# Ranking in pieces between VectorE's wide steps, with bucket numbers compared from PSUM, in a two-layer graph kernel

## The reference

```python
h = relu(layernorm(x))
x = x + segment_sum((h * node_vec1)[src], dst, 12500) * node_vec1_n2                     # layer 0
h = relu(layernorm(x))
x = x + (1 + eps) * h + segment_sum(relu(h[src] + edge_attr_32), dst, 12500)             # layer 1
```

## Time and profile before

| | us |
|---|---|
| median of 3 runs | 4801.34 |
| lowest, highest | 4799.08, 4803.71 |
| the profiled execution | 4791.23 |
| its span, first to last instruction | 4789.2 |

### The profile page before, as it was taken

One profiled execution on the slowest core, in us unless ns is written; L12 is line 12 of the kernel. 1 busy time (PEld: TensorE's weight loads), 2 busy tenths in 40 slices (PEclk: granted clock), 3 DMA queues, 4 the chain that ended last, 5 costly groups with the idle time before them and its releaser, 6 DMA issues.

```text
span 4789.2 us, 130194 instructions
## 1 busy us (share of the span) xinstructions
PE 3721.2 (78%) x43852; PEld 2888.9 (60%) x43852; DVE 3812.7 (80%) x11454; ACT 3261.3 (68%) x9090; POOL 3497.5 (73%) x3590
## 2 busy tenths in 40 slices
PE   0388888888888888888888899467767777777775
PEld 0266666666666666666666666356666666666664
DVE  9788888888888888888888886767777776777775
ACT  1377777777777777777777777456666766666664
POOL 6757777777777777777777777477777777777774
PEclk9999999999999999999999999778888888888887
DMA  6322222222222222222222221211212221211221
GB/s 111 63 51 54 57 54 54 54 56 54 54 54 56 54 53 54 56 54 53 54 56 54 53 54 44 72 39 54 57 43 54 57 57 54 58 49 48 57 57 26
DMA packets 439702, 262.77 MB, mean 55 GB/s; under 512 B 334660, under 2 KB 423732, under 8 KB 432632
## 3 DMA queue, kind: packets, MB, share of 16 engines
q1 hardware_dynamic: 322488, 187.55, 16.7%
q0 software_dynamic: 110816, 60.69, 6.7%
q10 hardware_dynamic: 5728, 5.82, 0.5%
HBM read 172.96 MB, written 80.85 MB: 53 GB/s over the span
## 4 chain that ended last, share of the span: by engine, by line
PE 32%; POOL 23%; DVE 19%; issue 13%; ACT 10%; DMA 2%; DVEq 1%; ACTq 0%; SPq 0%; POOLq 0%
POOL stage L759 22%; PE candidates L1247 18%; PE plain_ps L1259 7%; DVE arena L1753 7%; ACT message L987 5%; DVE arena L1729 4%; ACT centered L956 2%; PE sorted_agg L1187 2%; PE candidates L1157 1%; ACT arena L880 1%; POOL message L759 1%; PE key_rows L1230 1%; DMA stage<-in_edge_attr 1%; DVE counts L1475 1%; PE key_rows L1139 1%
## 5 line engine op out<-in xcount | busy, mean ns | idle before, releaser
L771 POOL DMA_INDIRECT records<-stage,place_i x1875 | 1879.0, 1002 | 696.2 <-issue 652.0
L759 POOL DMA_INDIRECT stage<-table,src_plain x1250 | 1246.9, 997 | 409.1 <-issue 377.3
L987 ACT ACTIVATE message<-candidates,member_is 128x96 bf16<-128x96 f32 x4560 | 1170.7, 377 | 429.4 <-PE candidates L1247 426.3
L1753 DVE TENSOR_SCALAR arena<-window_iota,dst_rel 128x224 bf16<-128x224 f16 (+1 forms) x4800 | 1091.2, 302 | 37.8
L880 ACT ACTIVATE arena<-key_rows 125x640 f16<-125x640 f16 x1000 | 653.2, 716 | 215.1 <-DVE arena L1729 83.2
L1187 PE MATMUL sorted_agg<-arena 128*96 128x224 bf16 (+1 forms) x5000 | 654.1, 285 | 161.0 <-DVE arena L1753 109.6
L1259 PE MATMUL plain_ps<-summed,message 128*96 128x224 bf16 x4560 | 609.2, 269 | 68.2 <-ACT message L987 68.2
L1187 PEld LDWEIGHTS sorted_agg<-arena 128*96 128x96 bf16 x5000 | 543.7, 137 | 186.1 <-issue 118.6
L1259 PEld LDWEIGHTS plain_ps<-summed,message 128*96 128x96 bf16 x4560 | 490.7, 128 | 269.6 <-ACT message L987 127.4
L1729 DVE TENSOR_SCALAR arena<-arena,row_key 125x1280 bf16<-125x1280 f16 x1000 | 554.7, 555 | 96.5 <-ACT arena L880 64.6
L1139 PE MATMUL key_rows<-ident,record 128*125 128x128 f16 x5000 | 425.8, 235 | 239.2 <-DMA record<-records 96.2
(11 more groups left out here) (228 smaller groups left out, 5139.0 us busy)
## 6 DMA issues: line engine op xcount, KB each, us to landing
record<-records SPq DMA_DIRECT2D x50, 1650.0 KB
stage<-in_edge_attr SPq DMA_DIRECT2D x125, 400.0 KB, 3.2
records<-pad SPq DMA_DIRECT2D x25, 1650.0 KB, 11.9
records<-stage,place_i POOLq DMA_INDIRECT x1875
stage<-table,src_plain POOLq DMA_INDIRECT x1250
message<-table,mid_src POOLq DMA_INDIRECT x288
xs<-in_x SPq DMA_DIRECT2D x8, 390.6 KB
table<-parts ACTq DMA_DIRECT2D x4, 585.9 KB
```

The lines of the kernel that those rows point to most:

```text
L759: pool.indirect_dma_start(message[:, k, j, :] if l == 0 else rows[:, k, j, :], None, table0 if l == 0 else table1, bass.IndirectOffsetOnAx ...
L771: pool.indirect_dma_start(records, bass.IndirectOffsetOnAxis(ap=place_i[:, h, e:e + 1], axis=0), stage[:, h, e, :], None).then_inc(scatter ...
L987: last = nc.scalar.activation(direct_message[n % DB][:, m * WIDE:(m + 1) * WIDE], candidates[n % 2][:, m * WIDE:(m + 1) * WIDE], ACT.Copy, ...
L1753: last = nc.vector.tensor_scalar(dst_onehot(g, t), window_iota[:, 0:WA if tile == 0 else WT], dst_rel[:, h, tile:tile + 1], None, ALU.is_e ...
```

## The change

`rank_within` is split in two for the batches of the loop. `rank_buckets` (the small steps and the three comparisons) follows step 2's `direct_onehots`, `rank_scans` of one unit each follows those of steps 2, 3 and 4, and `rank_sums` and `rank_places` follow those of step 6, ahead of the last wide step. TensorE's `prefixes` moves from ahead of step 6 to ahead of step 5. The bucket numbers that the comparison reads were float16 in SBUF and are now float32 in PSUM, in 75 columns of a bank that layer 0 uses for nothing but the scans' constant operand. To make room there, the scans go over 17, 17 and 16 buckets where they went over 20, 20 and 10; there are nine as before.

```diff
-        bucket16 = sb("bucket16", [P, SE], F16)
...
-        SCANNED = 20
+        SCANNED = 17
         goes_on = sorted_agg[1][:, 0:SCANNED * J]
+        bucket_ps = sorted_agg[1][:, SCANNED * J:SCANNED * J + SE]
...
-                            if n == FIRST[SUBS - 2] and left_after(b) >= 2:
+                            if n == FIRST[SUBS - 3] and left_after(b) >= 2:
                                 prefixes(b + 2)
...
             def rank_within(b, h, u):
+                rank_buckets(b, h, u)
+                for v in range(SORTED):
+                    rank_scans(b, v)
...
-                step(nc.vector.tensor_copy(bucket16[:], bucket_of[:]))
+                step(nc.vector.tensor_copy(bucket_ps, bucket_of[:]))
...
                     step(nc.vector.tensor_tensor(
                         in_bucket[:, v, :].rearrange("p (g j) -> p g j", j=J), bucket_iota[:],
-                        bucket16[:, v * J:(v + 1) * J].unsqueeze(1).to_broadcast([P, BUCKETS, J]), ALU.is_equal))
...
+                        bucket_ps[:, v * J:(v + 1) * J].unsqueeze(1).to_broadcast([P, BUCKETS, J]), ALU.is_equal))
...
+            def rank_scans(b, v):
...
+                for some in SCANS:
+                    last = nc.vector.tensor_tensor_scan(counts[:, v, some], goes_on[:, 0:some.stop - some.start],
+                                                        in_bucket[:, v, some], 0.0, ALU.mult, ALU.add)
...
                             direct_onehots(b, h, s)
-                            if s == SUBS - 3 and more:
-                                rank_within(b + 2, h, u + 1)
-                        if more:
-                            rank_sums(b + 2)
-                            rank_places(b + 2, h, u + 1)
+                            if s == 2 and more:
+                                rank_buckets(b + 2, h, u + 1)
+                            if s in (2, 3, 4) and more:
+                                rank_scans(b + 2, s - 2)
+                            if s == SUBS - 2 and more:
+                                rank_sums(b + 2)
+                                rank_places(b + 2, h, u + 1)
                         first_onehots(*after(b, h, u))
```

More of the change, by code:

```diff
@@ L1429, in rank_within, with rank_buckets @@
             def rank_within(b, h, u):
+                rank_buckets(b, h, u)
+                for v in range(SORTED):
+                    rank_scans(b, v)
+            def rank_buckets(b, h, u):
                 nth = [0]
@@ L1448, in rank_within, with step @@
                         in_bucket[:, v, :].rearrange("p (g j) -> p g j", j=J), bucket_iota[:],
-                        bucket16[:, v * J:(v + 1) * J].unsqueeze(1).to_broadcast([P, BUCKETS, J]), ALU.is_equal))
[L1450 to L1457, removed]
+                        bucket_ps[:, v * J:(v + 1) * J].unsqueeze(1).to_broadcast([P, BUCKETS, J]), ALU.is_equal))
+                assert nth[0] == 8 + SORTED
+            def rank_scans(b, v):
+                nth = [8 + SORTED + v * len(SCANS)]
+                def step(ins):
+                    nth[0] += 1
+                    ins.then_inc(rank1_steps, 1)
+                    dve.wait_ge(rank1_steps, b * RANK1 + nth[0])
+                for some in SCANS:
+                    last = nc.vector.tensor_tensor_scan(counts[:, v, some], goes_on[:, 0:some.stop - some.start],
+                                                        in_bucket[:, v, some], 0.0, ALU.mult, ALU.add)
+                    if v < SORTED - 1 or some != SCANS[-1]:
+                        step(last)
+                if v == SORTED - 1:
+                    last.then_inc(scans_ready, 1)
+                    assert nth[0] == RANK1
             HALVINGS = []
```

## The result

| | before | after |
|---|---|---|
| median of 4 runs each, us | 4802.32 | 4957.22 |
| lowest, highest | 4799.08, 4803.71 | 4954.49, 4963.40 |
| ratio | | 1.0325 [1.0307, 1.0343] |
| span of the profiled execution | 4789.2 | 4956.5 |

The change costs 155 us; forecast were 154. In the profile after, L1447 is L1452 (comparison), L1452 is L1465 (scans), L1475 is L1489 (sums), L1516 is L1530 (last of the places), L1729 is L1743, L1753 is L1767, L1808 is L1822 and L1819 is L1833. ScalarE's and TensorE's lines kept their numbers.

What follows compares the result with a forecast made beforehand. No engine is near its full span; VectorE and TensorE take turns in a batch of 114.70 us. Mean loss 6.5 us times 23 batches is 150, plus setup 3.7 and 10.1 from profiled to median: 4955 us, range 4890 to 5010.

Steps and rivals of the forecast that it cites:

- Scans cost nothing: VectorE's scans over 17, 17 and 16 buckets: 3077 ns a unit against 3076 before.
- The comparison: VectorE's comparison reading PSUM: 1454 ns against 837, so 1.85 us more a batch.
- Step 3 has its one-hots, barely: At step 3, eight of nine one-hots stand at 1076.4 us; TensorE wants the last pair at about 1076.7.
- VectorE stands 0.5 us earlier from step 6 on: From step 6, recovered waits of 2.33 us less 1.85 for comparisons put VectorE 0.5 us earlier.
- TensorE stands 5.8 us: At step 7, TensorE waits 5.8 us for one-hots held back by sums and places.
- The clock, 1.2 us: Behind the idle time at step 7, TensorE's clock falls to 0.5 and 1.2 us are lost.
- the upper end: High end of the range, 5010 us: longer slow stretch, a second behind the next first pick, dearer comparison.
- 6.0 us in one batch, 7.0 in the next, 23 times: Layer 0's batches lose 6.0 us on VectorE or, every second one, 7.0 on TensorE; mean 6.5, 150 in all.
- A batch that ends a set: At step 7 its lead is 7.8 us, so TensorE stands 7.3 us; it was given the same loss.
- Setup 3.7 us: The setup ranks two batches, each with 1.85 us more of comparison: 3.7 us.
- Rival 2: GpSimd sets the batch: earlier places gain 3.7 us a batch, 85 in all, giving 4716 us; chance 0.04.
- Rival 3: No change: step 7 is in time, which needs a lead of 16 us there; 4794 us; chance 0.05.

Runs made afterwards that it cites:

- Run 3: The changed kernel with bucket numbers kept as float16 in SBUF, so the comparison reads SBUF: 4902.64 us, 106.6 above the kernel before.
- run 4: The kernel before with only the comparison from PSUM and scans over 17, 17 and 16: 4829.91 us, 33.9 above the kernel before.
- run 1: The changed kernel with rank sums and places put back behind step 7: 4792.26 us, 3.8 below the kernel before.
- run 5: The changed kernel with 20 matmuls of unused result added on TensorE ahead of step 7: 4917.32 us, 116.2 above the kernel before.
- run 6: The changed kernel with the next batch's first two groups of keys turned and copied four tiles earlier: 4855.83 us, 54.7 above the kernel before.
- run 8: The changed kernel with sums and places behind step 7 and the comparison from SBUF: 4793.12 us, 8.0 below the kernel before.

## Why the prediction was right

The mechanism and its place held, and the size of the whole with them. Several of its terms were off, and the total came out partly because they cancel. By its steps:

- **Scans cost nothing.** 1044 and 990 ns, forecast 1043 and 991.
- **The comparison.** 1457 ns, forecast 1454 from the addition of PSUM prefixes. The Trainium skill ("VectorE: DVE Perf Modes", the section on the TRN2 errata) gives the estimates 1427 from PSUM and 711 from SBUF. Runs show 1457 and 837 to 841, and the row was the better guide. Run 3 prices it at 48 us in the change, run 4 at 34 by itself.
- **Step 3 has its one-hots, barely.** Right that it fits: its one-hots start 1.9 us ahead of TensorE (1131.08 and 1132.98; forecast 1.8), TensorE has no wait in the rows, and run 1 costs nothing.
- **VectorE stands 0.5 us earlier from step 6 on.** Mis-sized. The first row of the sums stands 1171.09 - 1160.63 = 10.5 us ahead of TensorE's arrival at step 7, where the earlier trace rows have 9.2: 1.2 us earlier. I had read the given-back waits from one batch (1.77 + 0.56). The two groups above show 51.8 + 12.8 = 64.6 us over 23 batches, 2.8 each, which leaves about 1 us after the comparison.
- **TensorE stands 5.8 us.** The first tile ends 5.7 us late: TensorE arrived at 1171.09 and would have been done at 1172.27, and is done at 1177.94. But 4.67 of it is idle and 1.0 is the tile's own longer time, since it starts on the first one-hots rather than on all five. Where run 5 kept the clock up the tile still took 1.51 us, so about 0.3 of this 1.0 is the pace of the one-hots and 0.7 the clock. On the mean the idle time is 5.25. (By its own terms the prediction's wait is 5.7, not 5.8.)
- **The clock, 1.2 us.** Under-sized: filling the wait gave back 1.7 us a batch. The slow stretch is 1176 to about 1181.5, and in this batch another follows at the next first pick; I had kept the second for the upper end only. It was no rare thing in the kernel before either: the first pick took 1.7 us or more in 12 of 25 batches there, and in 23 of 25 after.
- **6.0 us in one batch, 7.0 in the next, 23 times.** From the first pick of batch 0 (193.23 before, 197.28 after) to that of batch 23 (2890.26 and 3046.96) the loss is 152.7 us. That is 6.64 a batch over 23, against 6.5. But batch 22 loses nothing, so the other 22 lose 6.95 each: one batch less, each a little dearer, and that this comes out at the forecast is luck in part. The larger lead and the larger clock loss cancel as well. The two kinds of batches did alternate, by more than forecast: among batches 2 to 21 the odd ones lose 7.4 on the mean and the even ones 6.1, with single ones from 4.4 to 10.0. Whether the gaps named in the prediction are the reason was not tried. For the batch of the rows: idle 4.67, and step 7 to the next pick 12.81 us against 10.07, make 7.4, of which its group phase takes 0.6 back.
- **A batch that ends a set.** It was given the same loss, and has it: 6.8 us on the mean of five, 6.7 of the other 15.
- **Setup 3.7 us.** It is 4.05.
- **The rest.** Behind batch 23's first pick the profiled spans differ by 10.6 us more, 1898.9 and 1909.5. Kernels of this study that leave layer 1 alone spread over 1893 to 1914 there, so I put no cause to it.

Rival 2 (GpSimd sets the batch) is dead: GpSimd only waits more, 123.6 us for places in the waits after and 20.4 before, and the record load is issued 23 us before step 7, in the profile after:

```profile
1152.76 0.33 SPq L594 DMA_DIRECT2D record<-records  x1
```

Run 4 has the comparison from PSUM alone: GpSimd's 1875 scatters (L771) took 996 ns each there and 1002 before, 12 us in all, while the kernel lost 34. Whatever relief that is, no gain came of it. Rival 3 asked for a lead of 16 us; it is 10.5, and in the one batch that has 18.8 it came true.

The prediction did not see two things that the runs found. The second wait, VectorE's for ScalarE's keys, is not a mere consequence: turning the keys earlier removes two thirds of the loss (run 6), though part of that is the wait that they fill. And VectorE's lead at step 7 has a ceiling, the room `xs`, so the early pieces alone can't pay (run 8).

## What to carry to other kernels

Before work is moved ahead of another engine's input, read the lead at that very point, its start against the consumer's arrival, and compare it with the length of what is moved: 10 us held 9.9 of sums nearly for free and not 14.4, and 18.8 held all 14.4. A producer's lead is capped by the buffer that it must reuse; time that it saves beyond that cap is a gain only if something useful is put into the wait, and if the next thing that both sides need is moved up too. When two engines take turns, try to break the wait on each side: here two key turnings a few tiles earlier took back 100 of 155 us, with TensorE's wait at step 7 still 3.6 us in most batches. Moved too far, they wait for the next thing that they need, here the record load.

## What the runs showed of the hardware

- The clock has a price beyond the idle time: a standstill of 4.67 us was followed by 5 to 6 us at the granted clock 0.50 to 0.64 (stages from 1176 to 1182), and 20 matmuls with no use made the kernel 39 us faster.
- The same idle time did not always end the same way. In the kernel before, behind 2.39 us of idle time, the first pick took 1.02 us in one batch and 1.78 us in another:

```profile
886.21 1.78 PE L1157 MATMUL candidates<-parts,arena 125*128 125x96 bf16 x20 [2.39 <-ACT message L987]
```

In the batch of the earlier trace rows the clock fell as well, but only once the pick was over (1.00 up to 1124.50, 0.50 from 1124.60). What sets the moment of the fall was not settled.
- A comparison of 1250 float16 elements costs 837 to 841 ns with both inputs in SBUF and 1457 ns with one, of float32, in PSUM, almost exactly what an addition from PSUM costs (1454).
